# A two-layer transformer block on one core: the value products of the second attention layer in bursts of three pieces

## The reference, cut to what matters

```python
q = einsum('bld,dhk->blhk', x, Wq)                 # 16 heads of 64
latent = einsum('bld,dc->blc', x, Wkv_down)        # 32 channels
k = einsum('blc,chk->blhk', latent, Wk_up)
v = einsum('blc,chk->blhk', latent, Wv_up)
attn = einsum('bqhd,bkhd->bhqk', q, k) / sqrt(64)
attn = softmax(where(mask, attn, neg_inf))
y = einsum('bhqk,bkhd->bqhd', attn, v)
return einsum('bqhd,hdo->bqo', y, Wout)
```

## Time and profile before

| | |
|---|---|
| three runs | 2352.73, 2354.17, 2358.82 us, median 2354.17 |
| the profiled execution: span | 2342.6 us |
| median of the runs over that span | 11.6 us |
| PE busy | 2100.5 us (90%), 11754 instructions |
| PEld busy | 1367.6 us (58%) |
| DVE busy | 1553.7 us (66%) |
| ACT busy | 1379.9 us (59%) |
| POOL busy | 487.9 us (21%) |
| mean granted clock | 0.941 |

### The profile page before, as it was taken

The page is one execution under the profiler, slowest core; times in us unless marked ns, Lnnn a source line. Parts: engine busy times, 40 slices in busy tenths (PEclk is TensorE's granted clock), DMA queues, the critical chain, the costliest instruction groups (busy, mean ns, idle before and its releaser), DMA issues. The chain is left out here.

```text
span 2342.6 us, 45639 instructions
## 1 busy us (share of the span) xinstructions
PE 2100.5 (90%) x11754; PEld 1367.6 (58%) x11756; DVE 1553.7 (66%) x6216; ACT 1379.9 (59%) x2513; POOL 487.9 (21%) x808
## 2 busy tenths in 40 slices
PE   3489999999973999999977999999999997499998
PEld 2355555555543788888733555555555547378886
DVE  4388778877835677777755666666666633567776
ACT  1246666666663899999842555555555565355554
POOL 4101111111113000000000111111111110267666
PEclk9779999999995999999986999999999998599999
DMA  3523333323301221122167555555555521076553
GB/s 94 181 46 58 45 49 60 54 43 53 47 14 71 55 52 39 36 43 47 18 230 191 123 117 117 116 127 128 128 123 118 116 50 58 23 154 125 131 114 68
DMA packets 96653, 202.86 MB, mean 87 GB/s; under 512 B 14496, under 2 KB 32160, under 8 KB 96032
## 3 DMA queue, kind: packets, MB, share of 16 engines
q1 hardware_dynamic: 96544, 201.65, 38.9%
HBM read 169.47 MB, written 31.60 MB: 86 GB/s over the span
## 5 line engine op out<-in xcount | busy, mean ns | idle before, releaser
L570 DVE CUSTOM_DVE_ANT_0 a1ms<-a1S,mask_q 128x128 bf16<-128x128 f32 (+1 forms) x758 | 387.9, 553 | 182.8 <-issue 179.4
L624 ACT ACTIVATE a1p<-a1T 128x512 f32<-128x512 f32 x576 | 331.4, 597 | 293.8 <-PE a1T L724 293.3
L570 DVE CUSTOM_DVE_ANT_0 a0ms<-a0S,mask_q 128x384 bf16<-128x384 f32 (+2 forms) x752 | 385.8, 553 | 102.3 <-issue 96.9
L624 ACT ACTIVATE a0p<-a0T 128x512 f32<-128x512 f32 x576 | 330.7, 596 | 184.9 <-PE a0T L724 180.8
L703 PE MATMUL a1O<-a1p,a1v 128*33 128x512 f32 (+3 forms) x1536 | 304.2, 496 | 0.9 <-POOL a1p L538 0.9
L1177 DVE TENSOR_TENSOR m_hl<-m_h,m_hh 128x512 fp32r<-128x512 f32 x288 | 197.7, 690 | 116.6 <-ACT m_hh L1133 111.7
L724 PE MATMUL a0T<-a0qT,a0kT 128*128 128x512 f32 (+3 forms) x768 | 261.1, 391 | 3.3 <-DMA a0qT<-a0mr 2.9
L724 PE MATMUL a1T<-a1qT,a1kT 97*128 97x512 f32 (+3 forms) x768 | 262.8, 390 | 0.9 <-DMA a1qT<-a1mr 0.9
L663 PE MATMUL a0S<-a0kS,a0qS 128*128 128x384 f32 (+2 forms) x752 | 227.0, 361 | 32.1 <-DMA a0kS<-scr_k 26.3
L724 PEld LDWEIGHTS a1T<-a1qT,a1kT 97*128 97x128 f32 x768 | 131.6, 189 | 200.7 <-ACT a1p L624 144.5
L663 PE MATMUL a1S<-a1kS,a1qS 96*128 96x128 f32 (+1 forms) x758 | 220.5, 353 | 13.4 <-DMA a1kS<-scr_k 13.2
(11 more groups left out here) (234 smaller groups left out, 3642.4 us busy)
## 6 DMA issues: line engine op xcount, KB each, us to landing
m_gb<-scr_g SPq DMA_DIRECT2D x48, 1024.0 KB, 8.6
a1qS<-scr_q SPq DMA_DIRECT2D x96, 256.0 KB, 6.2
a1qT<-scr_q SPq DMA_DIRECT2D x96, 256.0 KB, 4.1
a1kS<-scr_k SPq DMA_DIRECT2D x96, 128.0 KB, 6.8
a1kT<-scr_k SPq DMA_DIRECT2D x96, 128.0 KB, 4.8
scr_q<-p_hi SPq DMA_DIRECT2D x32, 256.0 KB, 2.4
scr_q<-p_lo SPq DMA_DIRECT2D x32, 256.0 KB, 2.7
a0qS<-scr_q SPq DMA_DIRECT2D x48, 128.0 KB
```

Of the source, the lines that this page charges most:

```text
L570: nc.vector.tensor_tensor_reduce(masked_s[spare][:, 0:c1 - c0], buf[:, 0:c1 - c0], k.mask_q[:, SEQ - w + c0:SEQ - w + c1], 1.0, NEVER, ALU ...
L624: nc.scalar.activation(prob[p % PBUF][:, h, :], t_ps[slot % 2][:, :], ACT.Exp, scale=scale)\
```

## The change

`attention` takes three new parameters. `PARTS` was `HG // 2` and is now given: 2 in the first layer and 1 in the second, so both are as they were. `HALVES` stays at its default of 2 in both layers; with it every changed expression has its old value (`WIDTH` is 512, the new inner loop of the S unit runs once), and these hunks are left out below. `BURST` is 1 in the first layer and 3 in the second. There it puts the values of pieces 0 to 2 into slot 7, of 3 to 5 into slot 13, and of 6 to 8 into slot 1 of the next group, each three one after the other. The probability buffers become six, 4 KB more per partition for each of the three new ones, and `prob_of` picks the buffer by the piece's number over two groups, since 9 pieces are no multiple of 6. `COPY_0` follows the values of piece 4 and so moves from slot 12 to slot 14. `COPY_1`, the output transposes, the maxima and the S units stay in their slots.

```diff
-def attention(k, name, HG, VD, scale, operands, load_q, load_k, load_v, out):
+def attention(k, name, HG, VD, scale, operands, load_q, load_k, load_v, out, PARTS=1, BURST=1, HALVES=2):
...
-    PBUF = 3
-    assert NP % PBUF == 0
+    PBUF = 3 * BURST if BURST == 1 else 2 * BURST
+    assert NP % BURST == 0 and 2 * NP % PBUF == 0
...
-    DELAY, PARTS = HG, HG // 2
+    DELAY = HG
     VALUES, CARRIED = ({s: [] for s in range(NSLOT)} for _ in range(2))
     for p in range(NP):
         for part in range(PARTS):
-            s = p * HG + HG - 1 + DELAY + part * (HG // PARTS)
+            s = (p // BURST * BURST + BURST) * HG - 1 + DELAY + part * (HG // PARTS)
             (VALUES[s] if s < NSLOT else CARRIED[s - NSLOT]).append((p, part))
...
+        def prob_of(g, p):
+
+            return prob[(g[1] * NP + p) % PBUF]
+
...
-                            block_ = prob[p % PBUF][:, :, off:off + P]
+                            block_ = prob_of(g, p)[:, :, off:off + P]
...
-                            nc.scalar.activation(prob[p % PBUF][:, h, :], t_ps[slot % 2][:, :], ACT.Exp, scale=scale)\
+                            nc.scalar.activation(prob_of(g, p)[:, h, :], t_ps[slot % 2][:, :], ACT.Exp, scale=scale)\
...
-                                                    prob[p % PBUF][:, h, off:off + q1 - q0],
+                                                    prob_of(g, p)[:, h, off:off + q1 - q0],
...
-                          load_v0, attn)
+                          load_v0, attn, PARTS=2)
...
-                attention(k, "a1", 2, 32, 64.0 ** -0.5, rows, split_rows(q1, 2, 32, (0, 0, 1)), load_k1, load_v1, attn)
+                attention(k, "a1", 2, 32, 64.0 ** -0.5, rows, split_rows(q1, 2, 32, (0, 0, 1)), load_k1, load_v1, attn, BURST=3)
```

More of the change, by code:

```diff
@@ L365, in units_from @@
         return [(kind, h, i, half, ahead, min(n, NSLOT - 1)) for n, (kind, h, i, ahead) in enumerate(items)
-                for half in range(2 if kind == "o" or kind == "S" and i >= TPB // 2 else 1)]
+                for half in range(HALVES if kind == "o" or kind == "S" and i >= TPB // 2 else 1)]
     MAXIMA, NRED = {}, 0
@@ L372, in attention @@
         if kind == "S":
-            NRED += 3 if i == BLOCKS[-1] else 2
+            NRED += 3 if i == BLOCKS[-1] and HALVES == 2 else 2
             MAXIMA[h, i, half] = NRED
@@ L379, in attention @@
     START_MAXIMA = NRED + MAXIMA[start_units[-1][1:4]]
-    BANKS = 4
-    assert 2 * (NU + 2) % BANKS == 0
+    WIDTH = SEQ // HALVES
+    BANKS = 2 * HALVES
+    assert 2 * (NU + HALVES) % BANKS == 0
     base_items = own + [(*x, 2) for x in chain[:LEAD]]
-    DELAY, PARTS = HG, HG // 2
+    DELAY = HG
     VALUES, CARRIED = ({s: [] for s in range(NSLOT)} for _ in range(2))
@@ L414, in attention @@
         mhalf = [sb(f"mh{i}", [P, HG, TPB // 2], F32) for i in range(2)]
-        masked_s = [sb(f"ms{i}", [P, ST], BF16) for i in range(BANKS)]
+        masked_s = [sb(f"ms{i}", [P, WIDTH], BF16) for i in range(BANKS)]
         mrow = [sb(f"mr{i}", [TPB, HG, P], F32R) for i in range(2)]
@@ L420, in attention @@
         held = sb("held", [P, BANKS + NP], F32)
-        s_ps = [c.enter_context(nc.psum_tensor(name + f"S{i}", [P, ST], F32)) for i in range(BANKS)]
+        s_ps = [c.enter_context(nc.psum_tensor(name + f"S{i}", [P, WIDTH], F32)) for i in range(BANKS)]
         t_ps = [c.enter_context(nc.psum_tensor(name + f"T{i}", [P, ST], F32)) for i in range(2)]
@@ L430, in attention @@
         row_set = [[sem(name + f"row{i}{h}") for h in range(HG)] for i in range(2)]
-        banks = [*[t[:, :] for t in s_ps], o_ps[:, 0:ST], o_ps[:, ST:SEQ]]
+        banks = [*[t[:, :] for t in s_ps], *[o_ps[:, i * WIDTH:(i + 1) * WIDTH] for i in range(HALVES)]]
         start_ring = list(range(len(banks)))
@@ L447, in unit_base @@
         def unit_base(g):
-            return NU + NLEAD if at(g, 0) else lin(g, NU + 2, NU - 2 + (0 if at(g, NG - 1) else NLEAD))
+            return NU + NLEAD if at(g, 0) else lin(g, NU + HALVES, NU - HALVES + (0 if at(g, NG - 1) else NLEAD))
         def unit_slot(g):
-            return (NU + NLEAD if at(g, 0) else g[1] * (NU + 2) + NU - 2 + (0 if at(g, NG - 1) else NLEAD)) % BANKS
+            return (NU + NLEAD if at(g, 0) else g[1] * (NU + HALVES) + NU - HALVES + (0 if at(g, NG - 1) else NLEAD)) % BANKS
         def units_of(g):
@@ L553, in consume @@
                         if kind == "S":
-                            w, c0 = (i + 1) * P, half * ST
-                            c1 = min(w, c0 + ST)
-                            wide = w > ST
+                            w, c0 = (i + 1) * P, half * WIDTH
+                            c1 = min(w, c0 + WIDTH)
+                            wide = w > WIDTH
                             spare = bank % BANKS if ring is not start_ring else n % BANKS
@@ L572, in consume @@
                                                            ALU.add, ALU.max, found).then_inc(red_done, 1)
-                            if i == BLOCKS[-1]:
+                            if i == BLOCKS[-1] and HALVES == 2:
                                 dve.wait_ge(red_done, lin(gU, NRED, MAXIMA[h, i, half] - 1))
@@ L579, in consume @@
                             dve.wait_ge(unit_ready, base + (n + 1))
-                            rows = slice(half * TPB // 2, (half + 1) * TPB // 2)
+                            rows = slice(half * TPB // HALVES, (half + 1) * TPB // HALVES)
                             o = buf.rearrange("p (i h c) -> p i h c", h=HG, c=CT)
                             nc.vector.reciprocal(rec[par][:, rows, :], o[:, :, :, VD]).then_inc(rec_done, 1)
-                            dve.wait_ge(rec_done, lin(gU, 2, half + 1))
+                            dve.wait_ge(rec_done, lin(gU, HALVES, half + 1))
                             nc.vector.tensor_tensor(
                                 out[:, bass.ds(lin(gU, 1, 0), 1), rows, :].rearrange("p o i (h c) -> p (o i) h c", h=HG),
-                                o[:, :, :, 0:VD], rec[par][:, rows, :].unsqueeze(3).broadcast_to([P, TPB // 2, HG, VD]),
+                                o[:, :, :, 0:VD], rec[par][:, rows, :].unsqueeze(3).broadcast_to([P, TPB // HALVES, HG, VD]),
                                 ALU.mult).then_inc(out_done, 1)
@@ L591, in _ @@
                 main_steps(dve, lambda g: consume(units_of(g), unit_base(g), main_ring(unit_slot(g)), g))
-                consume(units_from([("o", 0, 0, 0)]), unit_base(END) + 2, main_ring(unit_slot(END) + 2), END)
+                consume(units_from([("o", 0, 0, 0)]), unit_base(END) + HALVES, main_ring(unit_slot(END) + HALVES), END)
             @block.scalar
@@ L599, in copy_out @@
                     if bank == 0 and not at(g, 0):
-                        act.wait_ge(out_done, lin(g, 2, 0))
+                        act.wait_ge(out_done, lin(g, HALVES, 0))
                     cols = slice(bank * ST, (bank + 1) * ST)
@@ L655, in unit @@
                         else:
-                            pe.wait_ge(out_done, lin(gP, 2, prev[3] + 1))
+                            pe.wait_ge(out_done, lin(gP, HALVES, prev[3] + 1))
                     buf = banks[ring[n % len(ring)]]
@@ L661, in unit @@
                             pe.wait_ge(ldS[gU[1]], gU[0] * (16 * NLOAD) + 16 * NLOAD)
-                        c0, c1 = half * ST, min((i + 1) * P, (half + 1) * ST)
-                        last = nc.tensor.matmul(buf[:, 0:c1 - c0], qS[gU[1]][0:SROWS, h, i * P:(i + 1) * P],
-                                                kS[gU[1]][0:SROWS, KI(h), c0:c1], start=True, stop=True)
+                        first = half * WIDTH
+                        for c0 in range(first, min((i + 1) * P, first + WIDTH), ST):
+                            c1 = min((i + 1) * P, c0 + ST)
+                            last = nc.tensor.matmul(buf[:, c0 - first:c1 - first], qS[gU[1]][0:SROWS, h, i * P:(i + 1) * P],
+                                                    kS[gU[1]][0:SROWS, KI(h), c0:c1], start=True, stop=True)
                     elif kind == "m":
@@ L669, in unit @@
                     else:
-                        pe.wait_ge(o_copied, lin(gU, 2, half + 1))
-                        for b in range(TPB // 2):
-                            rows = slice(half * ST + b * P, half * ST + (b + 1) * P)
+                        pe.wait_ge(o_copied, lin(gU, 2, (half + 1) * 2 // HALVES))
+                        for b in range(TPB // HALVES):
+                            rows = slice(half * WIDTH + b * P, half * WIDTH + (b + 1) * P)
                             last = nc.tensor.transpose(buf[:, b * P:(b + 1) * P], osb[:, rows], k.ident[:, :])
@@ L740, in _ @@
                         values(END, pv, part)
-                for n in range(2):
-                    unit(units_from([("o", 0, 0, 0)]), before(END)[2:], main_ring(unit_slot(END) + 2), n, END)
+                for n in range(HALVES):
+                    unit(units_from([("o", 0, 0, 0)]), before(END)[HALVES:], main_ring(unit_slot(END) + HALVES), n, END)
```

## The result

| | before | changed |
|---|---|---|
| median of 20 runs | 2355.26 us (2338.4 to 2365.1) | 2364.64 us (2350.9 to 2378.6) |
| ratio to before | | 1.0041, 95% interval 1.0023 to 1.0059 |
| profiled execution, span | 2342.6 us | 2363.0 us |
| PE busy, PEld busy | 2100.5, 1367.6 us | 2101.7, 1388.2 us |
| second attention loop, first T to last O | 652.5 us | 668.6 us |

The change makes the kernel slower by 9.4 us at the medians. The span of the changed kernel's profile is 1.7 us under the time of the same execution (2363.0 and 2364.7), so the 11.6 us that I put around the span were mostly the difference of two executions of before.

The account below looks back on a forecast made before the run. TensorE, busy 90% of the span, was taken as the bound. 2342.6 + 7.0 for full groups + 3.1 for the ends = 2352.7 span; plus 11.6 to the median, 2364 us. Range 2357 to 2374; 8 in 10, 2338 to 2379.

Parts of the forecast that it names:

- The entry cost: TensorE, second attention layer: each entry into and exit from value products costs about 0.32 us; six fewer save 1.92 a group.
- The loop of two slots: Two score buffers: scores to exponential 0.61, exponential 0.60, end to next weight load 0.05; 1.26 us for two slots.
- the stretch 8-14: TensorE between the transposed scores of slots 8 and 14: forecast to go from 6.54 to 6.51 us with waits.
- Copies at slot 14, banks: Slots 14 to 1: copies delay exponential 15, 0.65 us wait; VectorE's banks cost 0.22 and 0.12; stretch 7.40 us.
- rival (b): Copies behind exponential 14 and bank waits cost nothing: a group keeps 0.85 us more, 19.9, total 2340; chance 0.13.
- The sum of a group: Second attention layer, three stretches together: 20.71 us, taken as 0.24 us a group more, +7.0 over 29 full groups.
- What was put at nothing: Waits for earlier values, GpSimd's masks, the next group's loads and the maxima's store: each put at 0.
- The ends: First and last groups of the second attention layer: together +3.1 us.
- Group 30: Next-to-last group: no scores at slots 15 to 17, so its transposed scores wait bare, +0.9 us.
- Group 31: Last group, no scores to make: exponentials run apart from values, 21.9 us against 18.0, +3.9.
- Group 0: First group: no values to carry in and a later first burst, -1.7 us.
- The clock rival: Waits lower TensorE's clock once in 40 us: +1.2 us a burst, 16 times, +20 on the forecast, 2384; chance 0.08.

Follow-up runs that it names:

- e4: Changed kernel with both second-layer exponentials over 256 of 512 columns and maxima over a quarter of their columns: 19.21 us a group, loop 614.9 us.
- e1: Kernel before the change, with second-layer exponentials over 256 of 512 columns: 20.50 us a group, loop 653.0 us.
- e2: Changed kernel with second-layer exponentials over 256 of 512 columns: 20.33 us a group, loop 650.0 us.
- e3: Changed kernel with second-layer maxima taken over a quarter of their columns, exponentials whole: 20.31 us a group, loop 651.8 us.
- e5: Changed kernel with the bank-0 copy moved from slot 14 to behind the exponential of slot 1 of the next group: 20.53 us a group, loop 661.6 us.
- e6: Changed kernel with ScalarE's two waits before a piece's first exponential swapped, the buffer's first: 20.58 us a group, loop 661.1 us.
- e7: Changed kernel with values of the first and last groups in single pieces, bursts between: 20.73 us a group, loop 661.0 us.
- e8: Changed kernel with the edits of e5, e6 and e7 together and the S units moved to other slots: median 2336.76 us, ratio to before 0.994.
- e9: Kernel before the change with six probability buffers in the second layer, values still in single pieces: ratio 1.0015, loop 653.1 us.

## Why the prediction was right

**The entry cost.** 0.32 us an entry, 1.92 a group. Within a burst a piece of 512 columns follows the last at 0.85 to 0.89 us, and e4 shows 0.62 for two entries where next to nothing waits. Right.

**The loop of two slots.** 1.26 us was the sum's term; T8 to T10 is 1.27 in the profile after. With shorter exponentials the changed kernel moves and the one before does not (e1, e2). Right. Missed was that at T2 the first term becomes 0.53 or 0.70 by the parity of the group; before the change it is 0.62 in both, and it was luck that the 0.61 that I took is also their mean. In the stretch 8-14 two errors of the sum cancel: T10 to T12 was put at 1.27 and is 1.19, and the wait for the bank was put at 0.08 and is worth 0.16 in e3.

**Copies at slot 14, banks.** The stretch was put at 7.40 and is 7.40. e5 shows that the copy and the banks share the wait: each term, 0.65 and 0.34, is right only while the other stands. I gave rival (b) a gain of 0.85 if both were gone. e4 takes 0.79 or 0.62 out of this stretch and leaves the copy in its place, with shorter exponentials around it.

**The sum of a group.** Predicted +0.24, measured +0.27. Right.

**What was put at nothing.** Between 1330 and 1900 us TensorE's list of waits in the changed kernel has no DMA. Its weight loads waited for GpSimd's masks 3.9 us in all (10.2 before), so these terms were rightly left out.

**The ends.** Predicted +3.1, measured about +8. Group 30 was put at +0.9 and is +0.8 (20.21 against 19.38). Two terms were wrong. Group 31 was "21.9, +3.9" and is 25.1, +7.1: its working holds, as e6 shows with 22.0, but it was done at the full clock, and in this group the clock falls. Group 0 was "-1.7" and is +0.1 (22.13 against 22.03, T0 to T0). It was worked as if the clock rose when it did before. Over the first 22 us of the loop the clock reads 0.75, where before it read 0.87 (0.85 in the window of the first row, which begins 0.7 us ahead of the loop). Before and changed:

```profile
1271.00:1292.50 21.50, 20.12 (x90) 10.76 (x92) 12.97 (x78) 10.31 (x20) 3.81 (x13) 0.85 0.22 53
```

```profile
1274.00:1296.00 22.00, 21.29 (x84) 12.28 (x84) 11.58 (x70) 10.42 (x20) 3.72 (x13) 0.75 0.18 39
```

The five profiles whose group 0 has single pieces (before, e1, e7, e8, e9) show the rise 5.6 to 7.7 us after the first T, and the seven with bursts there 8.3 to 11.0 us. From before to changed it is 5.3 us later; at half the clock that is up to 2.6 us of TensorE's time, an estimate, and covers the 1.8 that the term missed.

**The clock rival.** It was priced for the middle groups, where no profile shows a fall: 1.00 in each window there. It came true at the two ends instead, at a quarter of its price; a burst at the lower clock costs 1.7 us more there, not 1.2. Of the seven profiles with bursts in group 31 four show the lower clock there (both of the changed kernel, e3, e5) and three do not (e2, e4, e6). Of the five with single pieces there one does (e8) and four do not. Idle time of TensorE does not sort them: e6's last group has 2.9 us of 22.5 and no fall, e8's window above has 0.7 of 20 and a fall. The Trainium skill, "TensorE: Matmul & The Clock Gate", section "Loop structure matters more than you think", says that long waits between products bring the slow clock; the longest idle time of TensorE in the changed kernel's last group is 0.6 us, and the clock fell all the same. What decides stays open.

**The whole.** +10.1 us was forecast, 2364. The loop's own cost is +16. The first timing, +9.4 by its medians, flatters the forecast: the second gives +16 by its medians and +20 by its ratio. The sign and the group's cost were forecast by the right mechanism; that the total met the number to within 1 us was in part luck, as the ends cost 5 us more than forecast and the first timing came out below the loop's own cost.

## What to carry to other kernels

Where an engine is full, a cheaper order of its work is worth only what its neighbours' latency allows: write down the loop through each double buffer (product, exponential, next product) and compare it with the work that stands in between, before and after the move. Two waits that cover each other stay hidden when only one of them is taken away; take both away together once, and the floor shows. After grouping work, deal out the other units of the ring again and treat the first and last groups apart, since there the cover is thinnest.

## What was not expected

The order of two waits on one ScalarE instruction matters when its start is in a latency loop: with the value of the second wait computed in a register after the first had been met, the exponential of slot 2 started 0.70 us after its T, against 0.53 with the buffer's wait first. And the last group's bursts at the lower clock took 4.4 us against 2.7, although the granted clock had been 1.00 for over 600 us before and TensorE had been idle for at most 0.6 us at a time in that group.
